# Relu's output and the probabilities turned without TensorE, in a fused attention and mixture-of-experts layer

## The reference, cut to what matters

```python
h = relu(xn @ nm_w1 + nm_b1)                    # "hid" in the kernel
m = h @ nm_w2 + nm_b2
q, k, v = m @ q_w + q_b, m @ k_w + k_b, m @ v_w + v_b
# each query sees the keys from 32 before it to 32 behind it in its sequence
attention = softmax(q @ k.T / sqrt(128), over that band) @ v
s = sigmoid(xn @ gate_w.T)                      # 16 experts, the 8 best of s + bias are taken
combine = s of the 8 / their sum * 2.826, 0 for the others
experts = sum_e combine_e * ((silu(xn @ w_gate_e.T) * (xn @ w_up_e.T)) @ w_down_e.T)
        + the same for one shared expert with weight 1
```

## Time and profile before

| | |
|---|---|
| median of 3 runs | 696.75 us (696.69 to 696.85) |
| the profiled execution | 696.95 us |
| its span, first to last instruction | 695.2 us |
| mean granted TensorE clock | 0.999 of full speed |
| instructions | 10439 |
| DMA | 93.94 MB, mean 135 GB/s |

### The profile page before, as it was taken

How to read it: one execution, slowest core, us unless ns; L and a number is a source line. 1 busy time by engine, 2 the same in 40 slices (tenths; PEclk the granted TensorE clock), 3 DMA queues, 4 the chain that set the end, 5 groups by cost and what they waited for, 6 DMA issues and landing times.

```text
span 695.2 us, 10439 instructions
## 1 busy us (share of the span) xinstructions
PE 683.9 (98%) x3232; PEld 559.2 (80%) x3232; DVE 584.5 (84%) x1625; ACT 438.1 (63%) x874; POOL 443.0 (64%) x400
## 2 busy tenths in 40 slices
PE   8989999999999999999999999999999999999997
PEld 6768788888888888888888888888888888888886
DVE  7998888978888787888978889787888978788775
ACT  5756665657666576665657566576665667566573
POOL 4775667566666666667566666666667567665553
PEclk9999999999999999999999999999999999999999
DMA  7817347171752728337192653728347171642800
GB/s 264 184 48 209 96 110 226 47 228 61 163 173 75 222 71 180 127 102 234 41 229 66 142 194 68 223 76 201 104 107 229 36 238 48 143 163 32 228 1 16
DMA packets 84536, 93.94 MB, mean 135 GB/s; under 512 B 8320, under 2 KB 74624, under 8 KB 84480
## 3 DMA queue, kind: packets, MB, share of 16 engines
q1 hardware_dynamic: 84480, 93.28, 48.9%
HBM read 88.49 MB, written 4.77 MB: 134 GB/s over the span
## 4 chain that ended last, share of the span: by engine, by line
PE 91%; DVE 5%; ACT 2%; issue 1%; DVEq 0%
PE ps_u L442 26%; PE ps_y L452 26%; PE ps_g L432 25%; PE bank L413 3%; PE bank L374 3%; PE bank L396 3%; PE ps_y L422 2%; PE bank L403 1%; PE bank L379 1%; DVE ps_u L1071 1%; PE bank L385 1%; PE ps_u L474 1%; DVE h_lo L1077 1%; ACT h_hi L684 0%; DVE silu_c L1058 0%
## 5 line engine op out<-in xcount | busy, mean ns | idle before, releaser
L1196 POOL TENSOR_TENSOR silu_c<-silu,comb_b 128x512 f32<-128x512 f32 x252 | 325.3, 1293 | 232.0 <-ACT silu L676 228.3
L684 ACT ACTIVATE h_hi<-ps_u 128x512 fp32r<-128x512 f32 x272 | 162.8, 599 | 243.9 <-DVE ps_u L1071 243.6
L1077 DVE TENSOR_TENSOR h_lo<-ps_u,h_hi 128x512 fp32r<-128x512 f32 x272 | 186.0, 684 | 48.0 <-ACT h_hi L684 44.4
L1071 DVE TENSOR_TENSOR ps_u<-silu_c,ps_u 128x512 f32<-128x512 f32 x256 | 176.5, 690 | 29.5 <-PE ps_u L442 25.2
L676 ACT ACTIVATE silu<-ps_g 128x512 f32<-128x512 f32 x272 | 162.0, 596 | 0.2
L442 PE MATMUL ps_u<-xn_hi,exp_w_hi 128*128 128x512 f32 x272 | 111.0, 408 | 4.1 <-DVE h_lo L1077 4.0
L452 PE MATMUL ps_y<-h_hi,exp_w_hi 128*128 128x512 f32 x272 | 110.4, 406 | 0.6 <-DVE h_lo L1077 0.4
L432 PE MATMUL ps_g<-xn_hi,exp_w_hi 128*128 128x512 f32 x272 | 107.7, 396 | 0.9 <-ACT silu L676 0.8
L442 PE MATMUL ps_u<-xn_hi,exp_w_lo 128*128 128x512 f32 x272 | 107.5, 395 | 0.0
L452 PE MATMUL ps_y<-h_lo,exp_w_hi 128*128 128x512 f32 x272 | 107.5, 395 | 0.0
L452 PE MATMUL ps_y<-h_hi,exp_w_lo 128*128 128x512 f32 x272 | 107.3, 394 | 0.0
(11 more groups left out here) (152 smaller groups left out, 988.1 us busy)
## 6 DMA issues: line engine op xcount, KB each, us to landing
comb_b<-c_dram SPq DMA_DIRECT2D x63, 1024.0 KB, 12.2
mom_b<-st_dram SPq DMA_DIRECT2D x13, 512.0 KB, 3.9
xres<-x_t SPq DMA_DIRECT2D x16, 256.0 KB, 2.7
out_t<-xres SPq DMA_DIRECT2D x16, 256.0 KB, 2.5
xin<-x SPq DMA_DIRECT2D x15, 256.0 KB, 3.0
xn<-x_t SPq DMA_DIRECT2D x13, 256.0 KB, 3.6
exp_raw<-wexp SPq DMA_DIRECT2D x3, 768.0 KB, 10.7
exp_raw<-wexp SPq DMA_DIRECT2D x2, 384.0 KB, 6.9
```

The lines of the kernel that those rows point to most:

```text
L684: A(h_t[hbuf(par, s)][0][:], ps_u[(par + s) % 2][:], ACT.Copy).then_inc(s_h_hi, 1)
L1071: V.tensor_tensor(ps_u[i][:], src[:], ps_u[i][:], ALU.mult).then_inc(s_h, 1)
L1077: V.tensor_tensor(t[1][:], ps_u[(par + s) % 2][:], t[0][:].bitcast(F32), ALU.subtract)\
L1196: G.tensor_tensor(silu_c[i][:].rearrange("p (l x) -> p l x", l=RUNS), silu[i][:].rearrange("p (l x) -> p l x", l=RUNS), comb_b[:, :, s1 - ...
```

## The change

1. `hid` of groups 1 to 15 is no longer turned by TensorE. `hid_relu` moves from step 13 to 11. VectorE turns the 32x32 blocks (`hid_blocks`, step 12) into `hid_b`; SP stores that by four DMAs to `h_dram` (`store_hid`) and loads it as one (`load_hid`) into `hid_m`, with its blocks in their places. `hid_n_hi` (now step 1), `hid_n_lo` (step 2) and `key_terms` read `hid_m`.
2. The probabilities of groups 1 to 15 are no longer turned by TensorE either. ScalarE scales them (`normalise_probs`, steps 6 and 7), VectorE turns 32x32 blocks (`prob_blocks`, 7 and 8) into `prob_b`, and twelve DMAs inside SBUF (`move_probs`, step 8, six before `spread_moments`' load and six behind) bring the blocks to other partitions, into `prob_m`. `prob_hi` is now in step 13 for both sequences, `prob_lo` in 14, `attend` in 15 and 16, `z_hi` and `z_lo` in steps 0 and 1 of the next group, `value_proj` in its step 2. In group 15 `prob_lo` is in 13, `attend` in 14 and 15, and `z_hi` and `z_lo` in 16.
3. `comb_b` lies as [expert, token] instead of in eight parts, and a spread has one run of 8 KB a partition. SP's order in step 12 is: store the combine weights, spread chunk 0, store `hid`, spread chunk 1, load `hid`, spread chunks 2 and 3.

`hid_b`, `hid_m`, `prob_b` and `prob_m` lie in the room of the raw expert weights, which is free after group 0; GpSimd clears `prob_m` once. VectorE's `moments` move from step 12 to 15 and `variance` from 13 to step 0.

```diff
+            def store_hid(g):
+                sp.wait_ge(S["hid_b"], g)
+                for t in range(4):
+                    sp.dma_start(h_dram[t * 32:(t + 1) * 32, :, :].rearrange("t q c -> q t c"), hid_b[:, t, :])\
+                        .then_inc(s_hid_st, 16)
+            def load_hid(g):
+                sp.wait_ge(s_hid_st, 64 * g)
+                if g > 1:
+                    sp.wait_ge(S["hn_lo"], g)
+                    sp.wait_ge(S["key_term"], 2 * g)
+                sp.dma_start(hid_m, h_dram).then_inc(s_hid_m, 16)
+            def move_probs(g, half):
+                sp.wait_ge(S["prob_b"], g)
...
+                for q in (2 * half, 2 * half + 1):
+                    for d in (-1, 0, 1):
+                        kq = (q + d) % 4
+                        src = prob_b[q * 32:(q + 1) * 32, :, (q + 1 + d) * 32:(q + 2 + d) * 32]
+                        if kq == q + d:
+                            dst = prob_m[kq * 32:(kq + 1) * 32, :, (q + 1) * 32:(q + 2) * 32]
+                        else:
+                            src = src[:, (d < 0)::2, :]
+                            c = 5 if d < 0 else 0
+                            dst = prob_m[kq * 32:(kq + 1) * 32, (d > 0)::2, c * 32:(c + 1) * 32]
+                        sp.dma_start(dst, src).then_inc(s_prob_m[q], 16)
...
             def store_comb(g, par):
                 sp.wait_ge(S["comb_t"], g + 1)
-                sp.dma_start(c_dram[par], comb_t[:]).then_inc(s_comb_st[par], 16)
+                sp.dma_start(c_dram[par].rearrange("e (l x) -> l e x", l=RUNS), comb_t[:])\
+                    .then_inc(s_comb_st[par], 16)
...
-                sp.dma_start(comb_b[:, :, c * CHUNK:(c + 1) * CHUNK, :].rearrange("p l e x -> p l (e x)"),
...
+                sp.dma_start(comb_b[:, c * CHUNK:(c + 1) * CHUNK, :].rearrange("p e t -> p (e t)"),
+                             c_dram[par].rearrange("(o e) t -> o (e t)", o=1)
+                             [:, c * CHUNK * T:(c + 1) * CHUNK * T]
+                             .to_broadcast([P, CHUNK * T])).then_inc(s_comb_b[c], 16)
...
                     if TURNED <= g + 2 < GROUPS:
+                        store_moments(g + 2)
+                    if not first(g):
+                        move_probs(g, 0)
+                    if TURNED <= g + 2 < GROUPS:
                         spread_moments(g + 2)
-                if s == 13 and not last(g):
+                    if not first(g):
+                        move_probs(g, 1)
+                if s == 12 and not last(g):
                     store_comb(g + 1, 1 - par)
-                    for c in range(NCHUNK):
+                    spread(g + 1, 1 - par, 0, False)
+                    store_hid(g + 1)
+                    spread(g + 1, 1 - par, 1, False)
+                    load_hid(g + 1)
+                    for c in range(2, NCHUNK):
                         spread(g + 1, 1 - par, c, False)
...
+                if s == 2 and not first(g):
+                    value_proj(g - 1)
                 if s == 15 and more:
                     q_proj(g + 1)
-                if s == 16 and more:
-                    hid_turn(g + 1)
...
             def hid_n_hi(g):
...
+                    act.wait_ge(S["pv"], g)
+                    act.wait_ge(s_hid_m, 16 * g)
+                    A(quarters(hid_n[0][:]), moved, ACT.Copy).then_inc(S["hn_hi"], 1)
...
+            def normalise_probs(g, seq):
+                act.wait_ge(S[f"inv{seq}"], g + 1)
+                for t in range(2):
+                    n = 2 * seq + t
+                    c = t * APART if first(g) else HALF + t * WIN
+                    done = A(prob_n[:, seq, c:c + WIN], prob[:, n, :], ACT.Copy, scale=row_inv[:, n:n + 1])
+                done.then_inc(S[f"pn{seq}"], 1)
...
             def prob_hi(g, seq):
...
+                    act.wait_ge(S["pv"], g)
+                    for q in range(4):
+                        act.wait_ge(s_prob_m[q], 48 * g)
...
+            def hid_blocks(g):
+                dve.wait_ge(S["hid"], g + 1)
...
+                V.transpose(hid_b.rearrange("p q c -> p (q c)"),
+                            hid[:].rearrange("p (a q t) -> p q a t", a=TILES, q=4)).then_inc(S["hid_b"], 1)
...
+            def prob_blocks(g, seq):
+                dve.wait_ge(S[f"pn{seq}"], g + 1)
...
+                done = V.transpose(within(prob_b, seq), prob_n[:, seq, HALF:HALF + 2 * WIN])
+                if seq == 1:
+                    done.then_inc(S["prob_b"], 1)
```

More of the change, by code:

```diff
@@ L26 @@
 APART = 3 * P - WIN
+BAND = 6 * HALF
 EPS = 1e-5
@@ L219, in layer @@
         S = {n: sem(n) for n in names}
+        s_hid_st = sem("hid_stored")
+        s_hid_m = sem("hid_loaded")
+        s_prob_m = [sem(f"prob_quarter_moved{i}") for i in range(4)]
         s_comb_st = [sem(f"comb_stored{i}") for i in range(2)]
@@ L571, in att_early @@
                     scores(1)
+                if s == 2 and not first(g):
+                    value_proj(g - 1)
                 if s == 15 and more:
                     q_proj(g + 1)
-                if s == 16 and more:
-                    hid_turn(g + 1)
             def att_late(g, par, s):
[L579 to L584, removed]
+                if first(g) and s == 12:
+                    pe.wait_ge(S["pn1"], 1)
+                    fresh_probs(1)
+                if s == (14 if last(g) else 15):
                     pe.wait_ge(S["hn_lo"], g + 1)
@@ L745, in att @@
                     prob_exp(g, 0)
-                if s == when(g, 7, 10):
+                if s in (when(g, 6, 9), when(g, 7, 10)):
+                    normalise_probs(g, s - when(g, 6, 9))
+                if s == when(g, 13, 10):
                     prob_hi(g, 0)
-                if s == when(g, 9, 12):
+                if s == when(g, 13, 12):
                     prob_hi(g, 1)
-                if s == 13 and more:
+                if s == 11 and more:
                     hid_relu(g + 1)
-                if s == 15:
+                if s == 15 and more:
+                    q_hi(g + 1)
+                if s == 16 and last(g):
                     z_hi(g)
-                    if more:
-                        q_hi(g + 1)
+                if s == 0 and not first(g):
+                    z_hi(g - 1)
             def slot(g, par, s):
@@ L1014, in att @@
                     route_match(g + 1)
-                if s == when(g, 10, 13):
+                if s == (13 if last(g) else when(g, 14, 13)):
                     prob_lo(g, 1)
@@ L1025, in att @@
                         variance(g + 2)
-                if s == 12 and TURNED < g + 3 < GROUPS:
-                    moments(g + 3, 1 - par)
+                if s == 0 and TURNED < g + 2 < GROUPS:
+                    variance(g + 2)
+                if s == 12 and more:
+                    hid_blocks(g + 1)
                 if s == 13:
@@ L1030, in att @@
                         moments(g + 2, par)
-                    elif g + 3 < GROUPS:
-                        variance(g + 3)
-                if s == 14:
-                    if first(g):
-                        variance(g + 2)
                     if more:
                         hid_lo(g + 1)
+                if s == 15 and TURNED < g + 3 < GROUPS:
+                    moments(g + 3, 1 - par)
+                if s == 14 and first(g):
+                    variance(g + 2)
+                if s == 1 and not first(g):
+                    z_lo(g - 1)
                 if s == 16:
-                    z_lo(g)
                     if more:
                         q_lo(g + 1)
+                    else:
+                        z_lo(g)
             def fresh_att(s):
@@ L1210, in slot @@
                         centre(g + 2, 1)
+                if first(g) and s == 14:
+                    clear_room()
                 if s == when(g, 2, 5):
```

121 lines of the change are left out of this document (79 added, 42 removed).

## The result

| | before | after |
|---|---|---|
| median, runs beside each other | 696.80 us (696.69 to 698.99, 4 runs) | 728.44 us (725.61 to 729.95, 4 runs) |
| ratio, 95% interval | | 1.0445 (1.0427 to 1.0464) |
| profiled execution, span | 696.95, 695.2 us | 729.95, 728.2 us |
| mean granted TensorE clock | 0.999 | 0.991 |
| c_dram's store to the next, steady groups | 41.8 us | 44.4 us (12 groups, 94.64 to 627.87) |

The account below looks back on a forecast made before the run. TensorE, busy 98% of the span, was taken as the bound. 696.95 - 16.5 (turns) + 7.5 (given back) - 1.0 + 1.0 (ends) = 687.95, less 0.2 for the median: 687.7 us, range 679.5 to 706.

Parts of the forecast that it names:

- I price the route at nothing: Relu's output through memory, steps 11 to 1: load lands at 401.3, 1.2 us before its limit, so costs nothing.
- about 0.45 with its gap: SP's issue of each of the twelve moves of the probabilities, taken from issues of other DMAs: about 0.45 us.
- third rival: Moves or fuller steps hold ScalarE or VectorE, a microsecond more a group, 703 us; moves from 0.17 us per issue; chance 0.12.
- 402.5: Latest harmless arrival of Relu's output, so that key_terms and h_lo of step 0 precede up_proj of step 2 at 403.8.
- The stores' movement: Four stores to h_dram: 1.5 us of movement; with few engines used up to 6, giving 737 us, or 692 at half.
- 1.10 us a group: TensorE's turns of hid and prob_n removed in 15 groups: 16.5 us saved together.
- 15 x 0.5 = 7.5 us is given back: ScalarE's scalings in steps 6 and 7 delay h_lo; TensorE waits 0.5 us a group at up_proj of step 8.
- transposes of 0.55 and 0.79: VectorE's block transposes, estimated us each; its load rises 0.45 us a group, 7 us in the run, priced at nothing.
- 6.3 us: Time for a 1 MB spread of the combine weights in long runs to land.
- -1.0 and +1.0: Group 0 gains 1.0 us by scalings moved to ScalarE; the last group loses 1.0 us by later z_hi and z_lo.
- Relu's output comes late: Load of hid_m waits behind stores and spreads; at the old spread pace 2.6 us late a group, 727 us; chance 0.22.
- Nothing is given back: ScalarE's scalings cost TensorE nothing: 680.3 us, down to 679.4; chance 0.20.

Follow-up runs that it names:

- e6: A with eight moves, the four moves of blocks to their own place left out, so part of the attention is not computed; 692.4 us.
- e14: A with the stores of Relu's output cut 32 outermost, eight moves issued and four same-place blocks copied by GpSimd; 691.39 us, ratio 0.9919.
- e3: B with only part 3 of the change, the spreads in long runs; 696.98 us, ratio 1.0000.
- e13: e11 with eight moves, four same-place blocks copied by GpSimd, and the scalings of the probabilities on VectorE again; 690.68 us, ratio 0.9909.
- A: The changed kernel, with all three parts of the change; 728.44 us, ratio 1.0445.
- B: The kernel before the change; 696.80 us.
- e9: A with z_lo ahead of key_terms in VectorE's step 1 and the stores of Relu's output cut 32 outermost; 697.9 us, ratio 1.0012.
- e11: e9 with hid_n_lo moved from VectorE's step 2 to its step 4; 701.29 us, ratio 1.0062.
- e7: A with the four stores of Relu's output issued ahead of the first spread; 724.48 us, ratio 1.0384.
- e1: B with parts 1 and 3 of the change, Relu's output through memory and long spreads, without the moves; 697.41 us, ratio 1.0006.

## Why the prediction was wrong

**The step that failed** is the arrival of Relu's output, "I price the route at nothing". From the moment at which the coefficients are ready (there 385.8, here 405.41):

| us | predicted | measured |
|---|---|---|
| SP free after the moves | 0.3 | 3.7 (to 409.12) |
| coefficients' store to the first spread | 1.4 | 2.6 (to 411.69) |
| first spread issued to stores landed | 7.8 | 8.2 (to 419.93) |
| to the load landed | 6.0 | 3.1 (to 423.05) |
| sum | 15.5 | 17.6 |
| limit | 16.7 | 15.9 |

- **The moves' issue, "about 0.45 with its gap", measured 0.64**: twelve are 2.3 us more. The rows behind it were of other DMAs. It is the largest error, and e6 and e14 show what it carries. The prediction had the threshold in its third rival, for the probabilities ("0.17 us more per issue"), and did not carry the same number on to the load behind.
- **From the coefficients' store to the first spread, taken as 1.4, there were 1.94** in the 13 other steady groups; the 2.6 of the table is of this group alone. The change scatters the far side of that store, and SP then needs 0.64 us to issue it, for 0.32 (0.59 in e3, where this is changed alone). The prediction took it as unchanged.
- **The limit "402.5"** took `h_lo` of step 0 as the first in need. In the order of the diff `z_lo` stands behind the `key_prod` and `value_proj` of step 2 needs it: TensorE was ready at 422.58, so with 0.6 us for two `key_prod` and 0.7 for `z_lo` the data had to land at 421.3, 0.8 us tighter than taken.
- **The stores' movement** had its rival, at the right place, with bounds that held the truth (2.1 us sooner with 32 outermost than with 4); but the forecast took the rival's cheap side. In the table their term is only 0.4 us over, since the spread ahead of them, 5.2 us here, was quicker than taken. The load went the other way: it landed 3.1 us after its issue, though a spread had been issued ahead of it at 414.58.
- Together, 1.2 us of slack became 1.7 us of lateness in this group, 1.5 in the five shortest waits and 2.1 in the mean of 13 (27.2 us); before the four longest, six of SP's moves took 4.1 to 5.2 us, for 3.8. What the lateness costs was over its own size: the granted clock fell behind some of the waits, which no rival had.
- **Turns, "1.10 us a group"**: the instructions are gone, and e13's 41.03 us is 0.35 over what this would leave of 41.78.
- **"15 x 0.5 = 7.5 us is given back" by the scalings on ScalarE**: the mechanism was right, and so was the place. The scalings and the late matmul of A:

```profile
396.03 0.74 ACT L764 ACTIVATE prob_n<-prob,row_inv 128x160 f32<-128x160 f32 x2
396.67 0.58 ACT L788 ACTIVATE h_hi<-ps_u 128x512 fp32r<-128x512 f32 x1
```

```profile
398.03 0.50 PE L525 MATMUL ps_u<-xn_hi,exp_w_hi 128*128 128x512 f32 x1 [0.18 <-DVE h_lo L1214]
```

  A pair takes 0.64 us from start to start (taken 0.62). In e14 1.10 - 0.49 = 0.61 us a group goes back (taken 0.5). But moving the scalings away returns only 0.26 of it (e13); VectorE then holds up other steps.
- **VectorE, "transposes of 0.55 and 0.79"**: 0.508 and 0.702. "I take nothing" for its sum holds in e14. What was missed are operations that it did before and that grew, `hid_lo` and `weight` below (mean ns behind the busy time); B has 692 and 279 for them.

```profile
L991 DVE TENSOR_TENSOR hid_lo<-hid,hid_hi 128x512 fp32r<-128x512 f32 x16 | 18.7, 1166 | 0.0
...
L966 DVE SCALAR_TENSOR_TENSOR weight<-rest,score 128x64 f32<-128x64 f32 x16 | 10.7, 669 | 0.1
```

- **The spreads, "6.3 us"**: 5.2 for the first of a group in A, 7.2 as the median of all. Right, and worth nothing by itself (e3).
- **Ends, "-1.0 and +1.0"**: group 0 is 2.6 us shorter in e14 (34.4 us between the first two stores, for 37.1), but group 1 is 2.1 longer (43.0 for 40.9) and the end 0.7. e14 gains 11 x 0.49 = 5.4 us in its steady groups and 0.1 in all the rest, where the forecast counted four groups more at 0.6. That and the 0.11 a group make up its 3.7 us over 687.7.
- **Rivals**: "Relu's output comes late" is what happened. That 728 lies beside the form priced at 727 is luck: that form had the old pace of the spread and 2.6 us a group, and no such pace was seen; what ran was SP's lateness and the slow stores together, 2.1 us a group, with the clock lost on top. "Nothing is given back" is out: no version reached 680. "The moves hold ScalarE": in A `p_hi` waits for them in 13 groups, 15.0 us in all and 3.2 at the longest, where the prediction had 2 us to spare. What that costs A by itself is not shown; in e9 to e11 it goes with the long groups.

## What to carry to other kernels

Price the issue of small DMAs by a row of their own kind, or by both sides of the nearest one, and follow SP's queue to its end: each move's error counts for everything behind it, not for the moves alone. Take as a transfer's limit the first instruction queued behind its reader on that engine, not the reader. Where DMAs are cut by hand, look at the outermost size of both sides: here 32 for 4 was worth 26 us. Moving one transfer ahead of another on the same queue can pass the delay on, as e7 did. And where two parts of a change share a queue, measure them together, since both may be harmless apart.

## What the hardware did that was not expected

- VectorE's `hid_lo` and `hid_n_lo`, 128x512 with both operands in SBUF, grew by the time for which a product that GpSimd had begun earlier ran beside them, less about 0.13 us: 0.68 us with no overlap (`hid_n_lo` in A), 0.69 with 0.12 (`hid_lo` in B), 1.05 with 0.50 (`hid_n_lo` in e1), 1.24 with 0.69 (`hid_lo` in A, 14 groups alike); `weight` the same, 0.70 with 0.62 for 0.21 without. Where VectorE had begun first (A, `hid_lo` at 51.91) it took its 0.68, and GpSimd's product 1.69 for 1.30. The Trainium skill (SBUF — State Buffer, SBUF: two separate sides) has it that such an operation and one of GpSimd that reads SBUF shut each other out; the rows agree.
- SP took 0.64 us from one move inside SBUF to the next, and 0.76 to 0.82 in some groups, for 0.32 to 0.38 of the DMAs of the earlier trace rows. Four stores of 64 KB took 2.5 us to issue with 4 outermost and 1.9 with 32.
- Those stores, when they alone moved data and with 4 outermost, kept the 16 DMA engines busy by 0.28 in the mean (e7, 412.0 to 413.0 us, 78 to 84 GB/s).
- After a wait of TensorE the granted clock fell to 1.2 GHz in four places of A, with 0.43 us from start to start for 0.23: after waits of 1.98, 2.58, 3.78 and 1.76 us. It did not after others of 2.56, 2.62, 2.04 and 2.21. The length of the wait alone doesn't tell.
